# Attention's edge products as one fp32r matmul over four stacked high and low terms

## The reference, cut to what matters

```python
w_m = (efeat @ W_msg + b_msg).reshape(E, 16, 16)
w_a = (efeat @ W_attn + b_attn).reshape(E, 16, 16)
h_src = feat[src][:, :, None]
e1, e2 = w_m * h_src, w_a * h_src
ex = exp(e2 - segment_max(e2, dst)[dst])
attn = ex / segment_sum(ex, dst)[dst]
ft = segment_sum(e1 * attn, dst).sum(axis=1)
```

## Time and profile before

| | |
|---|---|
| median of 3 runs | 2709.7 us (2708.16 to 2709.81) |
| profiled execution | span 2774.5 us; the page gives no other time for it |
| TensorE busy | 2191.1 us, 79% of the span |
| VectorE busy | 2233.7 us, 81% |
| ScalarE busy | 1763.9 us, 64% |
| GpSimd busy | 1321.9 us, 48% |
| layer 1's sum | about 729 to 973 us |
| edge work of attention | about 1090 to 2706 us |

### The profile page before, as it was taken

One profiled execution on the slowest core, in us unless ns is written; L12 is line 12 of the kernel. 1 busy time (PEld: TensorE's weight loads), 2 busy tenths in 40 slices (PEclk: granted clock), 3 DMA queues, 4 the chain that ended last, 5 costly groups with the idle time before them and its releaser, 6 DMA issues. The chain is left out here.

```text
span 2774.5 us, 36642 instructions
## 1 busy us (share of the span) xinstructions
PE 2191.1 (79%) x7895; PEld 960.2 (35%) x7896; DVE 2233.7 (81%) x3857; ACT 1763.9 (64%) x6869; POOL 1321.9 (48%) x1141
## 2 busy tenths in 40 slices
PE   1688888898699984488888888888888888888870
PEld 0344444466455532123222222222222222222220
DVE  7799999314587702399999999999999999999996
ACT  6577777013111111588888888888888888888843
POOL 5000000405550002577767777677777777777704
PEclk9899999888899996588888888888888888888885
DMA  3000000205785431012222222222222222222214
GB/s 69 6 0 0 0 0 0 93 1 177 244 259 179 139 116 23 19 52 71 71 71 71 71 71 71 70 63 71 71 71 71 71 71 71 71 71 71 66 57 123
DMA packets 109221, 205.35 MB, mean 74 GB/s; under 512 B 38652, under 2 KB 66980, under 8 KB 103406
## 3 DMA queue, kind: packets, MB, share of 16 engines
q1 hardware_dynamic: 67278, 156.49, 16.0%
q0 software_dynamic: 41888, 48.19, 8.0%
HBM read 76.22 MB, written 128.34 MB: 74 GB/s over the span
## 5 line engine op out<-in xcount | busy, mean ns | idle before, releaser
L1803 POOL DMA_INDIRECT hs<-h_table,gix x860 | 1081.6, 1258 | 434.5 <-issue 241.8
L1914 ACT ACTIVATE e<-wps,hs 128x32 f32<-128x32 f32 x5632 | 1030.6, 404 | 227.5 <-PE wps L1844 158.9
L1844 PE MATMUL wps<-w_edge,ef 18*128 18x512 f32 x1760 | 578.8, 706 | 301.1 <-ACT e L1914 162.6
L1866 PE MATMUL slot_sums<-e,ident 128*128 128x512 f32 x1392 | 757.0, 694 | 8.5 <-DVE e L2018 7.0
L1866 PEld LDWEIGHTS slot_sums<-e,ident 128*128 128x128 f32 x1392 | 294.8, 223 | 489.0 <-issue 463.7
L1844 PEld LDWEIGHTS wps<-w_edge,ef 18*128 18x128 f32 x1760 | 159.3, 200 | 678.1 <-ACT e L1914 309.8
L526 ACT CAST edges<-acc 128x400 f32 x600 | 295.0, 492 | 102.0 <-PE acc L513 75.3
L509 PE MATMUL acc<-q_hot,lo_hot 128*128 128x400 bf16 x1200 | 307.4, 338 | 53.3 <-DVE q_hot L483 51.4
L1953 DVE TENSOR_TENSOR e<-wps,hs 128x2048 f32<-128x2048 f32 x132 | 301.6, 2285 | 54.9 <-remote 23.0
L551 POOL DMA_INDIRECT got<-in_edge_rows,start x64 | 65.1, 1018 | 543.9 <-POOLq L464 417.6
L483 DVE TENSOR_SCALAR q_hot<-qcol,qT 128x400 bf16<-128x400 bf16 x1200 | 290.5, 317 | 1.0 <-PE acc L513 0.9
(11 more groups left out here) (381 smaller groups left out, 1964.0 us busy)
## 6 DMA issues: line engine op xcount, KB each, us to landing
rows_state<-states SPq DMA_DIRECT2D x43, 1280.0 KB
rows_shift<-shifts SPq DMA_DIRECT2D x44, 640.0 KB
got_order<-edges_order SPq DMA_DIRECT2D x56, 256.0 KB
ef_order<-efT SPq DMA_DIRECT2D x56, 256.0 KB
hs<-h_table,gix POOLq DMA_INDIRECT x880
ef<-ef_order SPq DMA_DIRECT2D x44, 320.0 KB
edges_order<-got POOLq DMA_DIRECT2D x32, 256.0 KB
edges_order<-msg_parts POOLq DMA_DIRECT2D x24, 256.0 KB
```

The lines of the kernel that those rows point to most:

```text
L1803: nc.gpsimd.indirect_dma_start(out=hs[u][:, s, :], out_offset=None, in_=d["h_table"], in_offset=bass.IndirectOffsetOnAxis(ap=gix[u][:, s:s ...
L1844: nc.tensor.matmul(wps[:, bank, :], ef[u][k:k + KM, g * P:(g + 1) * P], w[k:k + KM, :], start=True, stop=True).then_inc(a_mult, 1)
L1866: ins = nc.tensor.matmul(sums[:, g % 2, :], ident[:, :], e[u][:, g * SLOTS + c, :], start=(c == 0), stop=(c == SLOTS - 1))
L1914: ins = nc.scalar.mul(e[u][:, s, at], wps[:, bank, at], hs[u][:, s, f:f + 1])
```

## The change

The four-pass fp32 product is replaced by one product in the type float32r. Both operands are split: the high part is the value written as float32r, the low part the value less the high one, again as float32r. Products of high and low features with high and low weights are stacked as 4 x 18 = 72 rows, so that one matmul adds all four terms.

In `layer1_sum` ScalarE's copy now writes `efT_high`, and VectorE subtracts it from `tr` into `efT_low` (`remainder`, one turn late, ahead of the degree sum). Each has one buffer. Both are stored, to `ef_high` and `ef_low`. TensorE's next transposes wait for the remainder (`y_low`) instead of the copy.

In `attention_edges` a block's features come in four loads of 18 rows with all four slots of a step side by side, and the weights are split on VectorE at the start and stacked by four DMAs. TensorE's order in the period is unchanged; only the rows and the type of its products differ. A reordering of semaphore names in `prepare_pairs` (L251 to L255) moves no instruction.

```diff
-        efT = [sb(f"efT{v}", [SLOTS * KE, TURN, P]) for v in range(2)]
+        high, low = (sb(n, [SLOTS * KE, TURN, P], F32R) for n in ("efT_high", "efT_low"))
...
-                        sp.dma_start(d["ef_order"][:, groups, :], efT[r % 2][:, :, :]).then_inc(u_stored[r % 2], 16)
+                        sp.dma_start(d["ef_high"][:, groups, :], high[:, :, :].bitcast(F32)
+                                     ).then_inc(u_stored, 16)
+                        sp.wait_ge(y_low, turn + 1)
+                        sp.dma_start(d["ef_low"][:, groups, :], low[:, :, :].bitcast(F32)
+                                     ).then_inc(u_low_stored, 16)
...
                                 if r or j > 0:
-                                    pe.wait_ge(y_evac, j * TURNS_IN_CHUNK + r)
+                                    pe.wait_ge(y_low, j * TURNS_IN_CHUNK + r)
...
-                        if r >= 2 or later:
-                            act.wait_ge(u_stored[r % 2], (j * 2 + r // 2) * 16)
-                        nc.scalar.copy(efT[r % 2][:, :, :], tr[:, :, :]).then_inc(y_evac, 1)
+                        if r or later:
+                            act.wait_ge(u_stored, j * (TURNS_IN_CHUNK * 16) + r * 16)
+                        nc.scalar.copy(high[:, :, :], tr[:, :, :]).then_inc(y_evac, 1)
...
+                        if turn:
+                            remainder(turn - 1)
...
+                def remainder(turn):
+
+                    dve.wait_ge(y_evac, turn + 1)
+                    if turn:
+                        dve.wait_ge(u_low_stored, turn * 16)
+                    nc.vector.tensor_tensor(low[:, :, :], tr[:, :, :], high[:, :, :].bitcast(F32), ALU.subtract
+                                            ).then_inc(y_low, 1)
...
+        TERMS = ("high", "low", "high", "low")
+        KS = len(TERMS) * KM
+        w_in = sb("w_edge", [KM, 2 * CH])
+        w_high, w_low = sb("w_high", [KM, 2 * CH], F32R), sb("w_low", [KM, 2 * CH], F32R)
+        w = sb("w_terms", [KS, 2 * CH], F32R)
-        ef = [sb(f"ef{u}", [P, BG * P]) for u in range(2)]
+        ef = [sb(f"ef{u}", [KS, SLOTS, BG * P], F32R) for u in range(2)]
...
-                for c in range(SLOTS):
-                    sp.dma_start(w[c * KE:c * KE + KM, :], io["w_edge"]).then_inc(a_w, 16)
+                sp.dma_start(w_in[:, :], io["w_edge"]).then_inc(a_w, 16)
...
-                    sp.dma_start(ef[u][:, :], ef_t[:, cols(b, BG * P)]).then_inc(a_ef[u], 16)
+                    for n, term in enumerate(TERMS):
+                        sp.dma_start(ef[u][n * KM:(n + 1) * KM, :, :].bitcast(F32),
+                                     ef_t[term][0:KM, :, cols(b, BG * P)]).then_inc(a_ef[u], 16)
...
+                sp.wait_ge(a_split, 2)
+                for n, part in enumerate((w_high, w_high, w_low, w_low)):
+                    sp.dma_start(w[n * KM:(n + 1) * KM, :].bitcast(F32), part[:, :].bitcast(F32)).then_inc(a_terms, 16)
...
-                    g, k = s // SLOTS, s % SLOTS * KE
-                    nc.tensor.matmul(wps[:, bank, :], ef[u][k:k + KM, g * P:(g + 1) * P],
-                                     w[k:k + KM, :], start=True, stop=True).then_inc(a_mult, 1)
+                    g, c = s // SLOTS, s % SLOTS
+                    nc.tensor.matmul(wps[:, bank, :], ef[u][:, c, g * P:(g + 1) * P], w[:, :],
+                                     start=True, stop=True).then_inc(a_mult, 1)
...
+                dve.wait_ge(a_w, 16)
+                nc.vector.tensor_copy(w_high[:, :], w_in[:, :]).then_inc(a_split, 1)
+                dve.wait_ge(a_split, 1)
+                nc.vector.tensor_tensor(w_low[:, :], w_in[:, :], w_high[:, :].bitcast(F32), ALU.subtract
+                                        ).then_inc(a_split, 1)
```

More of the change, by code:

```diff
@@ L16 @@
 F32 = mybir.dt.float32
+F32R = mybir.dt.float32r
 BF16 = mybir.dt.bfloat16
@@ L141, in program @@
             "start_wide": dram("start_wide", [GTOTAL + 1], F32),
-            "ef_order": dram("ef_order", [SLOTS * KE, GORDER, P], F32),
+            "ef_high": dram("ef_high", [SLOTS * KE, GORDER, P], F32),
+            "ef_low": dram("ef_low", [SLOTS * KE, GORDER, P], F32),
             "marks": dram("marks_wide", [P, GSTEPS * 2], F32),
@@ L250, in prepare_pairs @@
         tr = prep.enter_context(nc.psum_tensor("tr", [P, PAIR_TILES, 4, P], F32))
+        b_rows = [sem("b_rows0"), sem("b_rows1")]
+        b_gather = sem("b_gather")
         b_consts, b_cast, b_blank, b_ends, b_node = (sem("b_" + n) for n in "consts cast blank ends node".split())
-        b_loaded, b_x, b_pairs, b_gather, b_stripdma = (sem("b_" + n) for n in "loaded x pairs gather stripdma".split())
+        b_loaded, b_x, b_pairs, b_stripdma = (sem("b_" + n) for n in "loaded x pairs stripdma".split())
         b_dve, b_pe, b_last, b_coarse, b_groups = (sem("b_" + n) for n in "dve pe last coarse groups".split())
         b_fine, b_rank, b_after, b_nought = sem("b_fine"), sem("b_rank"), sem("b_after"), sem("b_nought")
-        b_rows = [sem("b_rows0"), sem("b_rows1")]
         with nc.Block() as block:
@@ L1204, in layer1_sum @@
         u_load = [sem("u_load0"), sem("u_load1")]
-        u_stored = [sem("u_stored0"), sem("u_stored1")]
-        y_turned, y_evac, y_copied, y_masked, y_moved = (sem("u_" + n) for n in "turned evac copied masked moved".split())
+        u_stored, u_low_stored = sem("u_stored"), sem("u_low_stored")
+        y_turned, y_evac, y_low, y_copied, y_masked, y_moved = (
+            sem("u_" + n) for n in "turned evac low copied masked moved".split())
         lent = parts[:, 1, :, :, :].rearrange("p t a n -> p (t a n)")
@@ L1266, in _ @@
                 sp.wait_ge(m_store, 16 * 2 * CHUNKS)
-                for s in u_stored:
-                    sp.wait_ge(s, 16 * CHUNKS * TURNS_IN_CHUNK)
+                for stored in (u_stored, u_low_stored):
+                    sp.wait_ge(stored, 16 * 2 * CHUNKS * TURNS_IN_CHUNK)
             @block.gpsimd
@@ L1367, in _ @@
                     chunk(j)
+                remainder(2 * CHUNKS * TURNS_IN_CHUNK - 1)
                 v = Line(dve, m_dve)
@@ L1725, in attention_edges @@
         GM = 16 * BLK
+        EF = 16 * len(TERMS)
         shifts_t = d["rows_shift"].rearrange("(p j) c -> p j c", p=P)
         states_t = d["rows_state"][0:GTOTAL, :].rearrange("(p j) c -> p j c", p=P)
-        ef_t = d["ef_order"].rearrange("k g p -> k (g p)")
+        ef_t = {n: d["ef_" + n].rearrange("(c k) g p -> k c (g p)", c=SLOTS) for n in ("high", "low")}
         src_t = src[:, :, :].rearrange("p g c -> p (g c)")
@@ L1889, in period @@
                     for_act(u, b, (13, 14, 15))
-                pe.wait_ge(a_w, 16 * SLOTS)
-                pe.wait_ge(a_ef[0], 16)
+                pe.wait_ge(a_terms, 16 * len(TERMS))
+                pe.wait_ge(a_ef[0], EF)
                 period(0, 0, None)
-                pe.wait_ge(a_ef[1], 16)
+                pe.wait_ge(a_ef[1], EF)
                 period(1, 1, None)
@@ L1897, in _ @@
                     for u in range(2):
-                        pe.wait_ge(a_ef[u], i * 16 + 32)
+                        pe.wait_ge(a_ef[u], i * EF + 2 * EF)
                         period(u, i * 2 + (2 + u), i * 2 + u)
```

3 lines of the change are left out of this document (1 added, 2 removed).

## The result

The changed kernel takes 2714.4 us (median of 20 runs, 2711.4 to 2717.5) against 2710.8 us before (20 runs, 2706.8 to 2715.3). The ratio is 1.0014, 95% interval 1.0007 to 1.0020: slower by 3.6 us, which lies within the 0.2% named above. The forecast was 21 us less. So the question is where the gain went.

A forecast was written before the change was run, and what follows sets the result against it. Attention was taken as a VectorE loop with two holes, only the first TensorE's. Attention -36, layer 1's sum +12 and attention's start +3 made -21 us, carried to the runs as 2689 us, range 2668 to 2719.

The forecast's parts named there:

- a hole of 0.88 us a block: Attention: VectorE's wait for TensorE's slot sums before a block's first accumulation; shortening it by 0.85 us in 42 blocks gives -36 us.
- The second hole: Attention: VectorE idles 0.51 us a block before L1973 for ScalarE's last reads; forecast to stay.
- rival D: Attention: both of VectorE's idle gaps go, saving 21 us more, 2668 us; chance 0.05.
- The chain: TensorE in attention, from a block's last single-slot product to its last group sum: ends 0.7 to 1.9 us earlier, net.
- add1: TensorE's sum of slot group 1 in attention: more of it at half clock, losing 1.2 us at most.
- The product: Attention's fp32r product takes one pass of 0.215 us at full clock, instead of four passes, 0.86 us.
- p4: Lone product between the sums of groups 1 and 0 in attention: loses three passes of 0.215, 0.64 us.
- Rival B: Attention: fp32r takes two passes and groups of four take 1.91 us; gain only 12 us, 2713 us; chance 0.12.
- rival C: Attention: TensorE's clock falls further, 2.7 us more in every hole, 113 us in all, 2838 us; chance 0.05.
- Layer 1's sum: Its 56 turns: 6 us for VectorE's subtraction and 6 us for the rest, +12 us, bounds +4 to +45.
- rival A: Layer 1's sum: each of 56 turns waits 0.8 us for a store, costing 45 us, 2722 us; chance 0.14.
- The start of attention: Loading, splitting and stacking weights starts TensorE 3.5 to 7.5 us later, of which 0 to 4 come through: +3 us.

The follow-up runs named there:

- attention-only kernel: Changed kernel with layer 1's sum as before, one store, all four feature terms loaded from that tensor, low feature part left out: 2684.8 us, ratio 0.9912.
- the repeated execution: The kernel of before, unedited, profiled a second time: profiled span 2713.0 us.
- this part alone: Layer 1's split and both stores as in the change, attention's four-pass fp32 products as before, on the high part: 2741.6 us, ratio 1.0123.
- the two buffers: Changed kernel with a second high and a second low buffer in layer 1's sum: 2703.8 us, 0.9970 of before.
- the two part kernels: The change's attention part alone, 2684.8 us, and its layer 1 part alone, 2741.6 us, against 2709.6 us for before in the same session.

## Why the prediction was wrong

**Attention: mechanism right, size too large, though within its bounds.** I took -36 from a hole of 0.88 us a block. In an execution that lies with the runs, all holes together are 0.52 us, and a block falls by 34.10 - 33.50 = 0.60: 42 x 0.60 = 25 us, which is also what the attention-only kernel gained. The step that failed is the size of the hole: I read the earlier trace rows from an execution 64.8 us longer than the runs and carried "the same microseconds" over, instead of asking which holes a faster execution could still have. The second hole, which I left as it was and rival D closed, is absent from the repeated execution; nothing was to be gained there. The chain itself shrank by more than the 0.7 to 1.9 us that I worked out, by 1.6 to 3.5 (12.5 to between 9.1 and 10.9): I had charged add1 with up to 1.2 us for the clock, and it takes 4.3 to 6.1 us where it took 5.8. What goes beyond the hole brings nothing.

**The product: right, but for p4.** One pass: in the kernel that issues each product twice they follow each other every 0.234 us (seven steps from 1442.95 to 1444.59). A group of four holds TensorE for 1.04 us from its start to the next work's (2018.61 to 2019.65), my estimate 1.05. The record's own 1.20 us is over the 1.1 that I had named as a sign of being wrong, but it runs 0.16 us into the next work. Rival B, two passes, is out, and stacking gave up no time that mattered: 1.20 us for 1.14. The lone p4 holds TensorE for 0.64 us and not for the 0.41 of my working, so it saves 0.41 us instead of 0.64.

**The clock: rival C did not come.** In the stretch of the earlier trace rows it was granted at 0.82 after, at 0.83 in the execution that I read, but at 0.80 in the repeated one. The sums as a whole became slower (707 ns a record instead of 677 in the repeated kernel), yet L2081 waits for none.

**Layer 1's sum: wrong, and this decided it.** My term was +12, 6 for VectorE's added work and 6 for the rest. The change shows +26 from the first copy to the last, and this part alone +32 us in the run. The step that failed is "a landing of up to 2.6 us is hidden ... so it is near": the same row of the trace had a 256 KB load at 3.0 us, above the 2.6 that I had just worked out, and I still charged nothing for it. The stores land in 3.1 and 3.3 us. From one copy to the next that makes 0.59 for the copy, 0.72 until its store is issued and some 3.1 until it lands: 4.4 us for 4.03. While GpSimd's gathers run (until 850 us) they land in 3.6 and 3.8 us, and a turn takes 5.0 us on average. That is rival A's mechanism, at 0.47 us a turn on average instead of its 0.8 (258.3 and 232.3 us over 55 intervals). I had bounded this term by +45, but the reach of the forecast alone, up to 2703, was summed with +12. VectorE as the bound, the 6 that I did charge, is refuted by the two buffers' turns of 3.9 to 4.1 us.

**The start of attention: +3 forecast, 0 found.** TensorE starts 10.3 us later behind the marks' load (15.5 us instead of 5.2 in the repeated kernel), more than my 3.5 to 7.5, and the first VectorE product 6.1 us later, counted from the first gather. But the second block waits for gathered rows anyway.

Against the forecast of 2689, the sum with measured terms is -25 + 26 + 0 = +1 us, or +7 with the two part kernels, around the +3.6 measured.

## What to carry to other kernels

When a change turns two buffers into one, add up the round trip (copy, wait until its store is issued, landing, next copy) and compare it with the turn; if a row of the trace shows a landing near the limit, charge the wait for every turn. Before a hole in a loop is priced, compare the profiled span with the runs: an execution some per cent longer can have holes that the others don't. Here a cost in a stage ahead of the loop was paid in full, because the engine that it held up (TensorE) had no idle time there, while a cost at the start of the loop was free, because the loop's second turn waited for something else.

## What the runs showed that I had not expected

Four terms on 72 rows were no slower than one on 18, and in the traces faster by 7 us: the granted clock stood at 0.82 with 72 and 0.80 with 18, and slot sums that neither version changes took 709 and 765 ns. The two kernels differ in the loads of the features too; whether the rows as such raise the clock was not tried by itself.

Issuing a store 0.56 us sooner, at the moment when another queue issues a load, gained nothing: the load landed later (3.5 us for 2.9), and so did the store. And a profiled execution can lie 62 us above its kernel's runs without any run near it; ScalarE had idle time there that nothing in the profile explains, and why is open.
